# Half 1's exponential and inverse root as powers on GpSimd, in a one-core macaron block

## The reference

```python
x = x + 0.5 * ffn(layernorm(x))
x = x + attn(layernorm(x))
x = x + 0.5 * ffn(layernorm(x))
# ffn: h = silu(x @ w1 * s1) * (x @ w2 * s2); h = gelu(h @ h1 * g1); h = gelu(h @ h2 * g2); h @ w3 * s3
```

```python
logits = gelu(gate_in @ gW1 + gb1) @ gW2 + gb2
probs = softmax(logits.reshape(b, Ln, H, P) / tau[:, None], -1)          # P = 5 paths
probs = probs * (1.0 - sum(eps, -1, keepdims=True)) + eps
o = einsum('blhp,blhpd->blhd', probs, paths)
o = o * rsqrt(mean(o * o, -1, keepdims=True) + 1e-05) * norm_w
return o.reshape(b, Ln, D) @ Wo
```

## Time and profile before

| | us |
|---|---|
| median of 3 runs | 442.1 |
| lowest, highest | 439.83, 442.9 |
| the profiled execution's own time | 442.02 |
| its span in the trace | 440.3 |

### The profile page before, as it was taken

How to read it: one execution, slowest core, us unless ns; L and a number is a source line. 1 busy time by engine, 2 the same in 40 slices (tenths; PEclk the granted TensorE clock), 3 DMA queues, 4 the chain that set the end, 5 groups by cost and what they waited for, 6 DMA issues and landing times.

```text
span 440.3 us, 9783 instructions
## 1 busy us (share of the span) xinstructions
PE 371.1 (84%) x4132; PEld 278.6 (63%) x4132; DVE 294.8 (67%) x461; ACT 277.7 (63%) x434; POOL 41.9 (10%) x103
## 2 busy tenths in 40 slices
PE   5599999999999998899488489366599687978996
PEld 3377776678866876799377376233267465556885
DVE  2796679628216845699696968667868696578433
ACT  4788956879677776383243265451576838558973
POOL 4000000000000100000788400000000000000000
PEclk9899999999999996889956889585999898989999
DMA  8900007400000000071600001600000000001001
GB/s 272 333 1 2 2 0 227 111 1 1 1 1 0 0 2 3 4 214 49 173 5 4 1 4 36 230 1 1 0 1 3 1 0 2 0 1 49 3 1 48
DMA packets 14325, 19.75 MB, mean 45 GB/s; under 512 B 960, under 2 KB 9152, under 8 KB 14272
## 3 DMA queue, kind: packets, MB, share of 16 engines
q1 hardware_dynamic: 14128, 18.94, 14.4%
q10 hardware_dynamic: 144, 0.01, 0.0%
HBM read 17.91 MB, written 1.05 MB: 43 GB/s over the span
## 4 chain that ended last, share of the span: by engine, by line
PE 58%; DVE 26%; issue 7%; ACT 7%; DMA 1%; DVEq 0%; SPq 0%; ACTq 0%
PE ps_a L723 11%; PE ps_a L724 11%; PE ps_a L827 8%; PE ps_a L894 2%; PE ps_a L884 2%; DVE arena L1074 2%; DVE arena L1071 2%; PE ps_d L794 2%; PE ps_d L858 2%; PE ps_a L917 2%; DVE acts L1121 2%; PE ps_d L724 2%; PE ps_d L723 2%; PE ps_d L894 2%; DVE hbuf L1116 2%
## 5 line engine op out<-in xcount | busy, mean ns | idle before, releaser
L723 PE MATMUL ps_a<-acts,w_f 128*128 128x512 f32 x256 | 103.6, 405 | 9.1 <-ACT acts L597 8.5
L724 PE MATMUL ps_a<-acts,w_f 128*128 128x512 f32 x256 | 101.7, 397 | 0.0
L723 PEld LDWEIGHTS ps_a<-acts,w_f 128*128 128x128 f32 x256 | 49.2, 192 | 22.6 <-ACT acts L597 10.2
L724 PEld LDWEIGHTS ps_a<-acts,w_f 128*128 128x128 f32 x256 | 49.2, 192 | 10.9 <-issue 0.7
L597 ACT ACTIVATE acts<-ps_a,vec 128x512 fp32r<-128x512 f32 x64 | 44.6, 697 | 0.0
L827 PE MATMUL ps_a<-xnp,conv_w 128*128 128x512 f32 x156 | 38.5, 404 | 0.0
L1140 DVE TENSOR_TENSOR acts<-gbuf,acts 128x512 fp32r<-128x512 f32 x32 | 21.6, 689 | 24.9 <-ACT acts L597 24.9
L1140 DVE TENSOR_TENSOR acts<-ghbuf,acts 128x512 fp32r<-128x512 f32 x32 | 21.2, 689 | 20.8 <-ACT acts L597 20.8
L827 PEld LDWEIGHTS ps_a<-xnp,conv_w 128*128 128x128 f32 x156 | 29.3, 188 | 8.2 <-issue 1.4
L987 DVE SCALAR_TENSOR_TENSOR arena<-ps_d,arena 128x512 f32<-128x512 f32 x16 | 11.0, 686 | 30.4 <-ACT arena L551 26.3
L594 ACT ACTIVATE gbuf<-ps_a,vec 128x512 f32<-128x512 f32 x32 | 22.3, 697 | 10.3 <-PE ps_a L724 10.2
(11 more groups left out here) (211 smaller groups left out, 778.5 us busy)
## 6 DMA issues: line engine op xcount, KB each, us to landing
toep<-in_fir SPq DMA_DIRECT2D x24, 288.0 KB, 6.5
w_in<-in_h SPq DMA_DIRECT2D x4, 1024.0 KB, 8.2
g_rows<-in_gW SPq DMA_DIRECT2D x4, 640.0 KB, 6.7
w_in<-in_w SPq DMA_DIRECT2D x6, 256.0 KB, 4.7
iobuf<-in_x SPq DMA_DIRECT2D x4, 256.0 KB, 6.5
toep<-in_taps SPq DMA_DIRECT2D x1, 768.0 KB, 6.7
y<-iobuf SPq DMA_DIRECT2D x3, 256.0 KB, 2.4
toep<-in_proj SPq DMA_DIRECT2D x1, 256.0 KB, 8.6
```

The lines of the kernel that those rows point to most:

```text
L723: e.matmul(bank, w, hi, start=start, stop=False)
L724: return e.matmul(bank, w, lo, start=False, stop=stop)
```

## The change

Half 1's exponential and inverse root leave ScalarE. GpSimd gets two `TENSOR_TENSOR` instructions with the operation power: e to the power of each of the 160 elements of a partition (L472 of the changed kernel), and the 32 mean squares of a partition to the power of minus one half (L475). Two constants are set for them at the start. VectorE's `prob` and `scale` of half 1 wait for GpSimd in place of ScalarE. ScalarE loads Gelu's table once behind the `up` layer of tile 1, and no other table until tiles 2 and 3. Half 0's steps are as before.

```diff
 V = dict(...
-         mtau=47, rt0=55, epsd=48)
+         mtau=47, e=27, mhalf=53, rt0=55, epsd=48)
...
 # gpsimd
             own(e.memset(vc("l2eps"), L2_EPS))
+            own(e.memset(vc("e"), math.e))
+            own(e.memset(vc("mhalf"), -0.5))
             own(e.memset(vc("rmseps"), RMS_EPS))
...
-            e.memset(vec[:, 53:54], 0.0).then_inc(S["pool_inv"], 1)
+            e.memset(vec[:, 54:55], 0.0).then_inc(S["pool_inv"], 1)
 
             e.wait_ge(S["path4"], G)
             e.wait_ge(S["pe_a"], A_AT[("window", 2, 15)] + 1)
             e.memset(st[:, :, :, 4 * P:32], 0.0).then_inc(S["st_zero"], 1)
+
+            e.wait_ge(S["dve_sub"], 2)
+            e.tensor_tensor(ex5[:, 1], vc("e").unsqueeze(2).to_broadcast([128, 32, P]), ex5[:, 1], ALU.pow
+                            ).then_inc(S["pool_exp"], 1)
+            e.wait_ge(S["dve_ms"], 2)
+            e.tensor_tensor(rt, var, vc("mhalf").to_broadcast([128, DH]), ALU.pow).then_inc(S["pool_rms"], 1)
...
 # scalar: late()
                 if kind == "soft":
                     e.wait_ge(S["dve_sub"], i + 1)
                     e.activation(ex5[:, i], ex5[:, i], ACT.Exp).then_inc(S["act_exp"], 1)
-                    preload(ACT.Gelu if i else ACT.Abs_reciprocal_sqrt)
+                    preload(ACT.Abs_reciprocal_sqrt)
...
                     e.activation(rt, var, ACT.Abs_reciprocal_sqrt).then_inc(S["act_rms"], 1)
-                    preload(ACT.Gelu if i else ACT.Sqrt)
+                    preload(ACT.Sqrt)
...
                     if s == ("up", 1, 1):
-                        late("soft", 1)
+                        preload(ACT.Gelu)
...
                         for k, n in FILL.get((kind, i, m), ()) if f else ():
-                            late(k, n)
+                            if k == "osq":
+                                late(k, n)
...
 # vector: late()
                 elif kind == "prob":
-                    e.wait_ge(S["act_exp"], i + 1)
+                    e.wait_ge(S["pool_exp" if i else "act_exp"], 1)
...
                 elif kind == "scale":
-                    e.wait_ge(S["act_rms"], i + 1)
+                    e.wait_ge(S["pool_rms" if i else "act_rms"], 1)
```

More of the change, by code:

```diff
@@ L1 @@
+import math
 from contextlib import ExitStack
@@ L279, in program @@
                  "pe_a act_a pe_d dve_d dve_lo act_hi act_sq act_t dve_xn xn_pad pad_zero "
-                 "act_ss act_nt dve_nrm eye_done l_turned pool_inv inv_done path4 state act_l nums summed act_osq "
+                 "act_ss act_nt dve_nrm eye_done l_turned pool_inv pool_exp pool_rms inv_done path4 state act_l nums summed act_osq "
                  "st_zero act_stat dve_stat act_norm path3 st_turned ld_h2 act_exp dve_sub mixed dve_ms act_rms "
```

## The result

| | before | after |
|---|---|---|
| median of 4 runs each, us | 442.5 | 464.5 |
| lowest, highest | 439.83, 443.51 | 462.91, 465.93 |
| the profiled execution | 442.02 | 463.82 |
| its span | 440.3 | 462.1 |

The ratio is 1.0518, with a 95% interval from 1.0482 to 1.0555: 5.2% slower. I had forecast 439.2 us in a range up to 448.5. The sign was wrong and the time lies far outside.

A forecast was written before the change was run, and what follows sets the result against it. No engine was taken to bound the whole; around half 1's exponential and root VectorE mostly held the chain. Gains of 0.3 and 2.5 us, together 2.8 off 442.02, gave 439.2 us, range 435.5 to 448.5.

The forecast's parts named there:

- part 2: Exponential on GpSimd, ahead of `prob`: estimated at 4 us, root at 1 us; gain at this first place 0.3 us.
- The high end: Upper estimate for a GpSimd power, thirty steps each as dear as a multiply: 14 us for 160 elements, 3 for 32.
- the slow rival: A long exponential delays `prob` and idles TensorE: 451.2 us with powers of 14 and 3 us; chance 0.26.
- The lock: VectorE's two-input instructions wait until a GpSimd instruction ends; without it the first place would gain 1.65 us, not 0.3.
- Part 1: ScalarE without the exponential: the first Gelu starts 1.40 us behind its table load, 1.65 us sooner, the first place's most.
- Part 3: Root on GpSimd, second place: `scale` waits for two L1140 and the root; gain 2.5 us, at most 3.5 without lock.
- R: The time of the inverse root's power on GpSimd, 32 elements per partition; forecast as 1 us.
- isn't late: At `wo`, behind `scale`: TensorE has two banks of `hid2` to do first, and ScalarE frees their banks 3.6 us sooner.
- a rival on its clock: TensorE's lower clock ahead of `hid1` and `wo` takes back the gain, 1.6 us a stretch: 442.4 us at worst; chance 0.08.
- The 447 us: Time given for an exponential of 10 us, using the skill's figure of about 6 us for freshly loaded code's first call.
- T: The time of the exponential's power on GpSimd, 160 elements per partition; forecast as 4 us.
- What costs nothing: Two memsets at the start, 0.1 us each ahead of `cent_w`, are covered by the input's transfer; uncovered they cost 0.3 us.

The follow-up runs named there:

- the multiplies: The changed kernel with a multiply in place of each of GpSimd's two powers; 436.91 us, ratio 0.9898 against the kernel before.
- early_exp: The kernel before, with the exponential's table loaded early, behind the last SiLU of up of tile 1; 438.67 us against 441.62, ratio 0.9945.
- root_only: Only the inverse root of half 1 on GpSimd, the exponential on ScalarE as in the kernel before; 444.27 us, ratio 1.0065.
- exp_only: Only the exponential of half 1 on GpSimd, the inverse root on ScalarE as in the kernel before; 460.46 us against 441.64, ratio 1.0439.
- seed_root: The kernel before with half 1's inverse root on VectorE, from the exponent's bits and one more Newton step; 440.48 us, ratio 0.9959.
- The run by itself: A separate kernel, computing none of the reference, that times GpSimd powers of several sizes; 0.549 us for one element, 0.159 for each more.

## Why the prediction was wrong

**The step that failed is the price of a power**, in part 2: "some 14 steps at 1.6 ns, 22 ns per element, hence 4 us and 1 us". It measured 159 ns per element. The high end of 88 ns was too low as well, so the range and the slow rival, which I put at 451.2 us, missed too. The error was in the anchor. I took it from GpSimd's multiplies, the nearest rows, but each further element costs a power a hundred times what it costs a multiply (159 ns against 1.6). What GpSimd does in that time no run shows. I built both ends from the multiply's price, the high one by a guess at thirty steps, and so called a bound what was only a second guess. No row bounded it from above, and the chance of a long power, 0.26, was too small for that.

**The lock, also in part 2, failed.** I took it from one row; it holds for a multiply and not for a power. What the runs show of a power is contention at the start: VectorE's first instruction 0.23 us longer, or the power itself some 0.4 us longer. With the measured price and no lock the rest of the walk gives the result: GpSimd starts 0.08 us behind the subtraction's end rather than my 0.18, and `prob` starts 0.03 behind the power. In before's times that is 341.48 + 0.08 + 25.87 + 0.03 = 367.46 against 347.76: 19.7 us, the table's 19.7.

**Part 1 was right**: the first Gelu 1.40 us behind its load, 1.65 us at most; the multiplies gave 1.64 us. The Trainium skill's 2.66 us for a switch ("ScalarE: Activation LUTs", "What ACT_TABLE_LOAD costs") found no support in any run; early_exp hid one load and gained 1.42.

**Part 3's structure was right**: `scale` starts behind the later of two L1140 and the root. The multiplies gave 3.56 us where I had at most 3.5 without a lock. With R = 5.80 the place loses 1.2.

**TensorE "isn't late", and a rival on its clock.** I looked only at whether TensorE would be late; it was early. Where ScalarE no longer does the root, TensorE gets to `wo` ahead of VectorE and waits: 4.54 us in the changed kernel, 6.14 in root_only, 2.35 and 2.36 with the root on VectorE, 1.43 with the multiplies. (It was 0.29 before, but 1.75 in exp_only too, where ScalarE does the root.) The rival's size (1.6 us a stretch) fits the 1.7 to 2.2 us behind `wo`, and its place, ahead of `wo`, was named; I had given it 0.08 and as the end of a gain, where it came as a second part of the loss, and in its trace took two thirds of seed_root's gain.

**The slow rival's mechanism happened**: the wait at `prob`. In it I expected L1121 to be held, which it was not; TensorE stood 16.2 us for lack of low parts. The 447 us given beside it for T = 10 take R as a quarter of T; with the forecast's R of 1 the same sum is 445.2.

**What costs nothing** held: with the two memsets, `cent_w` ended at 3.14 us in the changed kernel (2.69 + 0.45), and TensorE still started at 4.99, behind the input's transfer, against 5.01 before.

## What to carry to other kernels

An operation that no row of the trace shows has no upper bound from the rows of a cheaper one; measure it alone first, at two sizes. The run by itself would have decided the change. Moving a function to a free engine pays only if its time there is shorter than the slack until the result is read: here about 4.5 us at the first place and 1.2 at the second, against 25.9 and 5.8. A table load can be cheaper to hide than to avoid: here one added preload gave 1.42 of the 1.64 us that the emptied first place was worth. A root can be had on VectorE from integer bits and one more Newton step. And an engine that gets to a wait sooner than before is a change as well: TensorE's longer wait ahead of `wo` cost up to 2.2 us by its clock.

## What the runs showed of the hardware

- GpSimd's power of fp32 elements took 0.55 us for one element per partition and 0.159 us for each further one (up to 160 tried), the same for one to the power of one as for the input's squares, and the same for 32 partitions as for 128.
- A GpSimd multiply on SBUF held VectorE's two-input instruction for its whole length (4.0 in place of 0.69 us, three times). A power of 25.8 us held it for 0.23 us at most. Where VectorE's instruction had started first, a power of 32 elements took 5.80 and 5.82 us in place of 5.42, and a multiply of 32 took 0.62 where one of 31 took 0.26.
- VectorE multiplied and added on int32 data in 0.18 us for 32 elements, and the result served as the first value of an inverse root.
- With TensorE idle for 2.35 us ahead of `wo` the granted clock behind it was 0.58 in one kernel, and with 2.36 us it stayed at 1.00 in another; behind 1.75 us it was 1.00, behind 4.54 us 0.50 and behind 6.14 us 0.53. In each the matmuls just ahead of the gap had run at 1.00.
